# The first scatter pass of a four-layer graph network: gathered rows as two scaled fp16 halves, three fp16 products a step

## The reference

```python
h = jnp.maximum(_layernorm(x, axis=-1), 0.0)
x = x + _L0_gnn_ref(h, L0_gnn_W, src, dst, edge_weight)
...
    Z = jnp.matmul(X, W)
    msg = Z[edge_src] * edge_vals[:, None]
    agg = jax.ops.segment_sum(msg, edge_dst, num_segments=X.shape[0])
    return jax.nn.relu(agg)
```

## Time and profile before

| | us |
|---|---|
| median of 3 runs | 2899.67 (2898.48 to 2909.13) |
| the profiled execution | 2885.73 |
| its span, first to last instruction | 2884.3 |

### The profile page before, as it was taken

How to read it: one execution, slowest core, us unless ns; L and a number is a source line. 1 busy time by engine, 2 the same in 40 slices (tenths; PEclk the granted TensorE clock), 3 DMA queues, 4 the chain that set the end, 5 groups by cost and what they waited for, 6 DMA issues and landing times.

```text
span 2884.3 us, 38704 instructions
## 1 busy us (share of the span) xinstructions
PE 2492.9 (86%) x9907; PEld 1394.1 (48%) x9907; DVE 1824.2 (63%) x4557; ACT 615.0 (21%) x1144; POOL 1025.3 (36%) x1095
## 2 busy tenths in 40 slices
PE   7879888788888888999899999998898788887786
PEld 5534444443333234666555555564687633333332
DVE  7765569567577775667333334334777687776766
ACT  4554410000056662000000000001565200000000
POOL 0366666676634441000000000000101466666665
PEclk9899998988976778999999999998999799999989
DMA  6586665566535444344611111111655367676665
GB/s 164 170 242 180 183 177 157 152 185 179 164 44 107 63 64 78 87 119 115 192 48 58 55 57 56 55 33 50 173 138 158 107 192 208 205 234 191 192 196 168
DMA packets 157069, 389.13 MB, mean 135 GB/s; under 512 B 44859, under 2 KB 46260, under 8 KB 156881
## 3 DMA queue, kind: packets, MB, share of 16 engines
q0 software_dynamic: 72400, 232.34, 28.1%
q1 hardware_dynamic: 83798, 153.04, 21.3%
q10 hardware_dynamic: 683, 1.28, 0.2%
HBM read 333.81 MB, written 52.72 MB: 134 GB/s over the span
## 4 chain that ended last, share of the span: by engine, by line
PE 60%; DVE 18%; issue 9%; DMA 7%; another core or an unknown queue 2%; POOL 2%; ACT 1%; SPq 0%; DVEq 0%; ACTq 0%
PE banks L1879 19%; PE banks L2020 16%; PE banks L1845 7%; PE banks L2014 7%; PE banks L2197 4%; DMA ring<-edge_counts 3%; DMA ring<-table,src_t 2%; POOL ring L2364 2%; DVE spare L1064 2%; PE banks L1834 1%; DVE ring L1616 1%; DVE sel L1137 1%; DVE spare L1060 1%; DVE rstd L901 1%
## 5 line engine op out<-in xcount | busy, mean ns | idle before, releaser
L1879 PE MATMUL banks<-ring,sel 128*125 128x512 f32 x1682 | 890.1, 658 | 156.4 <-issue 102.4
L2299 POOL DMA_INDIRECT ring<-table,src_t x440 | 441.8, 1004 | 233.6 <-issue 103.6
L1879 PEld LDWEIGHTS banks<-ring,sel 128*125 128x125 f32 x1682 | 290.2, 200 | 469.5 <-issue 466.0
L2364 POOL DMA_INDIRECT ring<-table,src_t x401 | 385.9, 962 | 216.6 <-issue 95.6
L2020 PE MATMUL banks<-acc,ring 125*125 125x512 f16 x1900 | 437.9, 381 | 8.1 <-DVE ring L1265 6.6
L2342 POOL DMA_INDIRECT x<-table,src_t x25 | 24.1, 963 | 1119.6 <-ACT spare L1778 1113.8
L2020 PEld LDWEIGHTS banks<-acc,ring 125*125 125x125 f16 x1900 | 257.0, 137 | 161.7 <-issue 28.5
L1616 DVE TENSOR_TENSOR ring<-ring,banks 128x512 f32<-128x512 f32 x388 | 255.7, 682 | 115.7 <-DMA ring<-table,src_t 93.7
L2014 PE MATMUL banks<-spare 128*125 128x450 f16 x590 | 265.3, 516 | 47.8 <-DVE spare L1064 16.5
L1064 DVE TENSOR_SCALAR spare<-node_scores,flags 128x450 f16<-128x450 f16 x590 | 192.7, 356 | 65.2 <-PE banks L2014 57.5
L2332 POOL TENSOR_SCALAR spare<-node_scores,den 128x125 f16<-128x125 f16 x195 | 146.2, 767 | 175.2 <-PE banks L2014 175.2
(11 more groups left out here) (412 smaller groups left out, 3185.7 us busy)
## 6 DMA issues: line engine op xcount, KB each, us to landing
ring<-edge_counts SPq DMA_DIRECT2D x35, 683.6 KB
edge_counts<-big SPq DMA_DIRECT2D x175, 97.7 KB
ring<-table,src_t POOLq DMA_INDIRECT x841
sel<-edge_counts SPq DMA_DIRECT2D x11, 683.6 KB
acc<-dst_places SPq DMA_DIRECT2D x28, 256.0 KB
x<-dst_places SPq DMA_DIRECT2D x27, 256.0 KB
acc<-src_digits SPq DMA_DIRECT2D x28, 224.0 KB
x<-src_digits SPq DMA_DIRECT2D x27, 224.0 KB
```

The costliest lines, as they stand in the source:

```text
L1879: last = P.matmul(to, sel[:, n % SELS, :], rows, start=False, stop=True, skip_group_check=True)
L2299: G.indirect_dma_start(out=ring[:, i % RING, :], out_offset=None, in_=table[0][:, :], in_offset=bass.IndirectOffsetOnAxis(ap=src_t[:, i:i ...
L2364: G.indirect_dma_start(out=rows_at(i), out_offset=None, in_=table[1][:, :], in_offset=bass.IndirectOffsetOnAxis(ap=src_t[:, i:i + 1], axis ...
```

## The change

- `table[0]` has 1024 fp16 values a row instead of 512 f32: the row times a power of two, rounded to fp16, and what that leaves, rounded to fp16. The bytes are the same, and so is the gather.
- The power of two comes from a bound of the rows: ACT squares and sums the first weight matrix, a one-column product on PE spreads the sum, and seven short instructions on DVE (`row_scale`, `powers`) make the scale.
- ACT writes the high half with that scale (`z_high`), and DVE has a new instruction for each tile (`rows_rest`) that reads the bank again and writes the rest; `pj_out` now comes from it. It stands at the head of DVE's turn, six tiles behind the statistics, so the loop has one turn more.
- The edge weights are scaled too, by their largest magnitude (two DVE instructions over the edge list at the head of `step_tables`, a transpose and a one-column product on PE, a reduction and `weight_scale` on DVE), and are split into two fp16 halves (`w16`).
- The selection of a step is two fp16 matrices side by side, high and low weight, from one scalar-tensor-tensor instruction over 2 x 125 columns.
- PE makes three fp16 products a step: high weight with both halves of the rows, low weight with the high half.
- ACT undoes both scales when it takes a tile (`unscale`).
- The prologue's products rotate over banks 3, 6 and 7 till tile 20, then over 6 and 7, and the table pieces on PE come one turn later (`TABLES_AT` 15).

```diff
-        table = [nc.dram_tensor(f"table{n}", (N, D), F32, kind="Internal").ap() for n in range(2)]
+        table = [nc.dram_tensor(f"table{n}", (N, D) if n else (N, 2 * D), F32 if n else F16, kind="Internal").ap() for n in range(2)]
...
+        sel16 = sel_room[:, 0:SELS * TN].bitcast(F16).rearrange("p (s a n) -> p s a n", s=SELS, a=2)
...
+        ring16 = flat_ring.bitcast(F16).rearrange("p (r c) -> p r c", c=2 * D)
+        w16 = w_t[:, :].bitcast(F16).rearrange("p (i a) -> p i a", a=2)
...
+        THIRD_TILL = TILES - 4
+
+        def first_bank(t):
+
+            return bank[3] if t % 3 == 2 and t < THIRD_TILL else bank[6 + (t % 3 == 1 if t <= THIRD_TILL else (t - THIRD_TILL) % 2)]
+
+        def first_bank_free(t):
+
+            return t - 2 if t <= THIRD_TILL + 1 else t - 1
...
+            def powers(n):
+
+                own.mark(V.tensor_scalar(out=down[:, n:n + 1].bitcast(I32), in0=exponent[:, n:n + 1], scalar1=-float(1 << 23),
+                                         scalar2=float(268 << 23), op0=ALU.mult, op1=ALU.add))
+                own.mark(V.tensor_scalar(out=up[:, n:n + 1].bitcast(I32), in0=exponent[:, n:n + 1], scalar1=float(1 << 23),
+                                         scalar2=-float(14 << 23), op0=ALU.mult, op1=ALU.add))
+                V.wait_ge(v_own, own.n)
+
+            def row_scale():
+                V.wait_ge(w0_bound, 2)
+                own.mark(V.tensor_scalar(out=bound[:, 0:1], in0=bank[1][:, 0:1], scalar1=Z_NORM * Z_NORM, scalar2=1e-30, op0=ALU.mult, op1=ALU.max))
...
+                powers(0)
+                V.tensor_copy(bound[:, 0:1], down[:, 0:1]).then_inc(w0_bound, 1)
+
+            def weight_scale():
+                V.wait_ge(below, 3)
...
+                powers(1)
+                own.mark(V.tensor_tensor(unscale, up[:, 0:1], up[:, 1:2], ALU.mult))
+
+            def rows_rest(t):
+                V.wait_ge(z_high, t + 1)
+                V.scalar_tensor_tensor(out=z_halves_at(t)[:, D:2 * D], in0=first_bank(t)[0:TN, :], scalar=down[0:TN, 0:1],
+                                       in1=z_halves_at(t)[:, 0:D], op0=ALU.mult, op1=ALU.subtract).then_inc(pj_out, 1)
...
+                own.mark(V.scalar_tensor_tensor(out=dst_junk.rearrange("p (c e) -> p c e", c=EC), in0=edf[:, :, 2, :], scalar=-1.0,
+                                                in1=edf[:, :, 2, :], op0=ALU.mult, op1=ALU.max))
+                V.wait_ge(v_own, own.n)
+                own.mark(V.tensor_reduce(squares[0:EP, 1:2], dst_junk, axis=AX.X, op=ALU.max))
+                V.wait_ge(v_own, own.n)
+                yield
...
+                V.tensor_reduce(peak, bank[2][0:1, 0:128], axis=AX.X, op=ALU.max).then_inc(below, 1)
...
+                weight_scale()
...
-                V.tensor_copy(w_t[:, :], bank[2][:, 0:STEPS]).then_inc(tables, 1)
+                own.mark(V.tensor_scalar(out=scaled_w, in0=bank[2][:, 0:STEPS], scalar1=down[:, 1:2], scalar2=None, op0=ALU.mult))
+                V.wait_ge(v_own, own.n)
+                own.mark(V.tensor_copy(w16[:, :, 0], scaled_w))
+                V.wait_ge(v_own, own.n)
+                V.tensor_tensor(w16[:, :, 1], scaled_w, w16[:, :, 0], ALU.subtract).then_inc(tables, 1)
...
-            for n in range(TILES + 5):
+            for n in range(TILES + 6):
+                if 0 <= n - 6 < TILES:
+                    rows_rest(n - 6)
...
+                if n == 4:
+                    row_scale()
...
-                V.tensor_scalar(out=sel[:, i % SELS, :], in0=node_iota[:, :], scalar1=dl_t[:, i:i + 1],
-                                scalar2=w_t[:, i:i + 1], op0=ALU.is_equal, op1=ALU.mult).then_inc(sel_ok, 1)
+                V.scalar_tensor_tensor(out=sel16[:, i % SELS, :, :], in0=node_iota[:, None, :].to_broadcast([CE, 2, TN]), scalar=dl_t[:, i:i + 1],
+                                       in1=w16[:, i, :, None].to_broadcast([CE, 2, TN]), op0=ALU.is_equal, op1=ALU.mult).then_inc(sel_ok, 1)
...
-                        A.activation(acc[0:TN, t, :], bank[n][0:TN, :], ACT.Relu).then_inc(kept, 1)
+                        A.activation(acc[0:TN, t, :], bank[n][0:TN, :], ACT.Relu, scale=unscale[0:TN, :]).then_inc(kept, 1)
...
+                    A.activation(square_junk, raw_w0.rearrange("p k d -> p (k d)"), ACT.Square, accum_out=squares[:, 0:1]).then_inc(w0_bound, 1)
...
-                    A.copy(zbuf(t), bank[6 + t % 2][0:TN, :]).then_inc(pj_out, 1)
+                    if t == 0:
+                        A.wait_ge(w0_bound, 3)
+                    A.activation(z_halves_at(t)[:, 0:D], first_bank(t)[0:TN, :], ACT.Copy, scale=down[0:TN, 0:1]).then_inc(z_high, 1)
...
-                rows = ring[:, r, :] if layer < LAST else rows_at(i)
-                last = P.matmul(to, sel[:, n % SELS, :], rows, start=False, stop=True, skip_group_check=True)
-                if layer == LAST:
+                if layer < LAST:
+                    for a, half in ((0, 0), (0, 1), (1, 0)):
+                        last = P.matmul(to, sel16[:, n % SELS, a, :], ring16[:, r, half * D:(half + 1) * D], start=False, stop=True,
+                                        skip_group_check=True)
+                else:
+                    last = P.matmul(to, sel[:, n % SELS, :], rows_at(i), start=False, stop=True, skip_group_check=True)
...
-                    if t >= 2:
-                        P.wait_ge(pj_out, t - 1)
-                    project(t)
+                    if first_bank_free(t) > 0:
+                        P.wait_ge(pj_out, first_bank_free(t))
+                    P.wait_ge(pj_lo, t + 1)
+                    product(t % 2, first_bank(t)[0:TN, :], pj_z)
...
-                store_rows(t, zbuf(t))
+                store_rows(t, z_halves_at(t))
```

More of the change, by code:

```diff
@@ L1906, in tensor_program @@
                     P.wait_ge(counted, TILES - 1)
+                    P.transpose(bank[2][0:1, 0:128], squares[:, 1:2], ident[:, :])
                     P.matmul(bank[0][:, 0:TILES - 1], ones[0:EP, :], cnt[:, :], start=True, stop=True).then_inc(below, 1)
+                if n == PEAK_AT:
+                    P.wait_ge(below, 2)
+                    P.matmul(bank[2][:, 128:129], ones[0:1, :], peak, start=True, stop=True).then_inc(below, 1)
                 if n == TURNED_AT:
```

36 lines of the change are left out of this document (28 added, 8 removed).

## The result

The changed kernel is slower by 0.4%: 2917.7 us (median of 6 runs) against 2901.4 us for the kernel before on the same chip, ratio 1.0041, 95% interval 1.0027 to 1.0056. The forecast was 2868 us, range 2834 to 2908. One thing has to be said for the numbers that follow: in two of the six sets of runs everything was faster, the kernel before included (2728 and 2729 us in place of 2899 to 2906). I call these the second setting, and the others, with the profiles of before and after, the first; ratios are always taken inside a set. In the second setting the changed kernel costs more, 1.0110 [1.0084, 1.0135].

A forecast was written before the change was run, and what follows sets the result against it. The prediction took PE and POOL, which waits for the ring of 11 rows, as sharing the bound, with DVE in two stretches. The pass's -39 us and the prologue's +7 made -32: 2899.7 to 2868 us, range 2834 to 2908.

The forecast's parts named there:

- -22: First pass, 185 to 410 us: three quarters of POOL's 29.8 us of ring waits go, -22 us.
- -11: First pass, 510 to 635 us: three quarters of 14.6 us go, ring waits 8.4 and a table wait 6.2.
- -6: First pass, 710 to 790 us: three quarters of 7.4 us of ring waits go, -6 us.
- the end's -5: From last gather to last tile's copy, 10.8 us: a backlog of three or four rows, not a full ring, -5 us.
- The wait in the block of five: At L2294, 510 to 635 us: POOL stands 6.2 us for a DVE table; PE closer to POOL brings it earlier.
- VectorE where it is full: First pass, dearer selection without room: 410 to 510 us no gain, +5 us; 635 to 710 us, +2 us.
- Rival 5: Each gather waits out one selection, 1.25 + 0.48 = 1.73 us a gather: 2997 us, chance 0.04.
- the page beside it: Skill page on SBUF: a DVE instruction with two SBUF inputs contends with GpSimd, the loser blocks entirely; L876's row against it.
- the prologue: Before the first gather: more DVE work, mainly `rows_rest`, +5 us, and +2 at the end: +7 us, bounds 0 and +20.
- rivals 2, 5 and 6: The last of these: product's weight loads not hidden, 1.05 us a step against 0.89, 2926 us, chance 0.03.
- Rival 1: First pass: PE's granted clock falls with more idle time, ring waits stay, 2907 us or about 2895; chance 0.12.
- rival 2: First pass: DVE takes the pass, selection at 0.78 us, 2932 us, chance 0.11; a loss from 0.67 us a selection.

The follow-up runs named there:

- b_scratch2k: The kernel before with half the room for the descriptors of POOL's gathers, 2048 bytes a partition in place of 4096; ratio 1.0031, in the second setting.

## Why the prediction was wrong

- **The step that failed** is the reading of the earlier trace rows, that POOL's 89.3 us of waits are waits for the ring of 11 and that three quarters go with a cheaper product. It carried most of the gain: -22, -11, -6 and the end's -5. The waits are 80.0 us before and 83.9 after by my count, 87.1 with half the product, 82.7 with a third. That POOL stands at the ring was right; that the product's length holds the ring was not. A releaser named in a row says what came last, not what was slow.
- **The wait in the block of five** (6.2 us, so 4.7 of the -11) was laid to a table of DVE's that a closer PE brings earlier. It stayed, 6.5 us before and 6.4 after; b_scratch2k shows it as one for descriptors' room.
- **VectorE where it is full** was mis-sized, not misread: +5 and +2 against +8.5 (steps 200 to 260) and +4.7 (steps 300 to 440). The longer gathers of these steps, 3.2 us, are counted here and in the next term.
- **The gathers' own time** was held at 1.004 us in the sum. It went to 1.037 and 1.049, +14.3 and +20.5 us, the largest term. Rival 5 and the page beside it had the mechanism, at 0.48 us each; the size was a tenth of that or less. L876's row could not exclude it: it shows that VectorE isn't slowed, and says nothing of the gathers beside it.
- **The rest held.** Products stand 0.22 us apart; two steps take 1.50 us with the last one's tail:

```profile
331.11 1.50 PE L1954 MATMUL banks<-ring,sel 128*125 128x512 f16 x6
```

  The selection 474 ns (480 forecast), 0.134 us more back to back (0.13); the prologue +7.2 and +6.6 us (+7); the clock 0.85 to 0.90 in the windows from 185 us on, where it was 0.88 to 0.92. None of them could save the sum. A slip without effect: the chances of rivals 2, 5 and 6 add up to 0.18, not 0.17.
- **The rivals.** None named waits that stay while PE is light. Rival 1 gave a near time (2907) for a cause that isn't there, the clock. The turn to slower came as in rival 2, through VectorE, at the selection's expected size: its point of decision, 0.67 us, rested on gains that weren't there.

**What stays open.** Why `stepped` comes late in the first setting, so that POOL waits 80 us. It isn't the product's length, nor the ring's size. It comes and goes with the 0.7 us instructions on PE's queue and with PE's "issue" time; it grew in the one run that gave that queue more instructions, but inside the setting it does not follow their count. That is a pairing, and no run made the one without the other. What makes a setting isn't known.

## What to carry to other kernels

Before a wait is counted as a gain, make its supposed cause cheaper in one run, even with a wrong output: half a product settled here in one kernel what the profile could not. Where an engine issues gathers at a fixed pitch, take the pass apart into that pitch, the longer gathers and the waits; the pitch didn't move here in twenty profiles, and each term has its own cause. And see which gather of a block waits: the signal in the program may stand ahead of another. A cheaper operation on an engine that waits, paid with a dearer one on an engine whose work stretches the pacer's, was a loss in both settings.

## What the runs showed of the hardware

- Single instructions of PE's queue, a wait, a move or an addition, took 0.6 to 0.85 us in bursts in one setting (87 of 2257) and never in the other, and the same kernel differed by 6% (2901 and 2729 us), 69 us of it in this pass by the profiles.
- POOL's gather of 128 rows has a floor of 0.95 us and 0.30 to the next, in every kernel and setting, with rows of 2 KB and of 1 KB; a waiting instruction or four ahead of it cost nothing.
- Of five gathers of edge rows in a row (1.65 us each) the fifth waited 6.5 us with 4096 bytes a partition of room for descriptors; with 2048 the third waited 6.5 and the fifth 6.3.
- A gather is stretched by VectorE's work beside it: to 4.82 us at most, 0.03 to 0.05 us on the mean for a selection that reads two tensors.
